# A selective scan over sixteen states: four of sixteen B products move to ScalarE and TensorE

## The reference

```python
xc, z = split(x @ in_w.T); xc = silu(causal_conv4(xc) + conv_b)       # 128 channels each
dt, Bm, Cm = split(xc @ x_w.T)                                        # rank 4, 16 states, 16 states
dt = softplus(dt @ dt_w.T + dt_b); A = -exp(A_log)
dA  = exp(dt[..., None] * A)                                          # token, 128 channels, 16 states
dBx = dt[..., None] * Bm[:, :, None, :] * xc[..., None]
h_t = dA_t * h_{t-1} + dBx_t
y_t = sum_s h_t[:, s] * C_t[s]
y = (y + xc * D) * silu(z);  out = y @ out_w.T
```

## Time and profile before

| | |
|---|---|
| median of 3 runs | 2970.94 us (2959.31 to 2975.59) |
| profiled execution, its own time | 2967.89 us |
| its span, first to last instruction | 2966.1 us |
| busy over the span | PE 84%, POOL 70%, DVE 78%, ACT 53% |
| mean granted TensorE clock | 0.899 of full speed |
| forward direction | about 815 to 1722 us from the span's start |
| backward direction | about 1730 to 2692 us |

### The profile page before, as it was taken

One profiled execution on the slowest core, in us unless ns is written; L12 is line 12 of the kernel. 1 busy time (PEld: TensorE's weight loads), 2 busy tenths in 40 slices (PEclk: granted clock), 3 DMA queues, 4 the chain that ended last, 5 costly groups with the idle time before them and its releaser, 6 DMA issues. The chain is left out here.

```text
span 2966.1 us, 34800 instructions
## 1 busy us (share of the span) xinstructions
PE 2497.7 (84%) x7800; PEld 1190.2 (40%) x7800; DVE 2318.3 (78%) x2487; ACT 1576.8 (53%) x2784; POOL 2084.2 (70%) x1166
## 2 busy tenths in 40 slices
PE   7899999957468988889889858899889889988598
PEld 7666666624322323323323223333333333336422
DVE  4366666560659999999999939998999899895499
ACT  6466666543655655555656446555555555545221
POOL 3133333230359999999999949999999999995155
PEclk6699999969779999999999889999999999997599
DMA  3000000000256777777777637776766676660022
GB/s 60 8 9 9 9 9 9 6 1 0 59 167 223 243 244 237 247 235 240 246 236 241 227 124 235 219 236 216 229 226 222 221 225 224 218 211 17 13 54 47
DMA packets 177295, 437.72 MB, mean 148 GB/s; under 512 B 65638, under 2 KB 70219, under 8 KB 177228
## 3 DMA queue, kind: packets, MB, share of 16 engines
q1 hardware_dynamic: 139340, 420.19, 44.5%
q10 hardware_dynamic: 37888, 16.79, 2.1%
HBM read 404.40 MB, written 24.12 MB: 144 GB/s over the span
## 5 line engine op out<-in xcount | busy, mean ns | idle before, releaser
L1443 POOL TENSOR_TENSOR sb_hc<-sb_h,sb_cc 128x1024 f32<-128x1024 f32 x256 | 599.7, 2360 | 61.8 <-PE sb_py L1232 56.2
L1443 POOL TENSOR_TENSOR sf_hc<-sf_h,sf_cc 128x1024 f32<-128x1024 f32 x256 | 595.8, 2347 | 11.5 <-DVE sf_h L1521 8.2
L1232 PE MATMUL sf_py<-sf_hc,ident 128*128 128x512 f32 x1024 | 533.1, 655 | 0.6 <-POOL sf_hc L1443 0.6
L1232 PE MATMUL sb_py<-sb_hc,ident 128*128 128x512 f32 x1024 | 519.5, 638 | 0.0
L572 POOL TENSOR_TENSOR ar_sc<-ar_sc,ar_mx 128x512 f32<-128x512 f32 x128 | 154.7, 1208 | 356.6 <-DVE ar_mx L513 356.6
L1521 DVE TENSOR_TENSOR_SCAN sf_h<-sf_dA,sf_state,sf_pu 128x1024 f32<-128x1024 f32 x160 | 375.4, 2346 | 19.1
L1521 DVE TENSOR_TENSOR_SCAN sb_h<-sb_dA,sb_state,sb_pu 128x1024 f32<-128x1024 f32 x160 | 375.2, 2345 | 17.1
L1232 PEld LDWEIGHTS sf_py<-sf_hc,ident 128*128 128x128 f32 x1024 | 197.0, 205 | 269.3 <-issue 239.8
L1232 PEld LDWEIGHTS sb_py<-sb_hc,ident 128*128 128x128 f32 x1024 | 187.3, 196 | 241.0 <-issue 232.0
L1501 DVE TENSOR_TENSOR sb_pu<-sb_pu,sb_dtx 128x1024 f32<-128x1024 f32 x160 | 193.9, 1212 | 52.7 <-PE sb_pu L1212 52.7
L1436 POOL TENSOR_TENSOR sb_dbx<-sb_dtx,sb_bb 128x1024 f32<-128x1024 f32 x96 | 226.5, 2359 | 3.3 <-DVE sb_dtx L1482 3.3
(11 more groups left out here) (294 smaller groups left out, 4594.6 us busy)
## 6 DMA issues: line engine op xcount, KB each, us to landing
sf_cc<-rows_scratch SPq DMA_DIRECT2D x256, 512.0 KB, 4.4
sb_cc<-rows_scratch SPq DMA_DIRECT2D x256, 512.0 KB, 4.4
sf_bb<-rows_scratch SPq DMA_DIRECT2D x96, 512.0 KB, 5.4
sb_bb<-rows_scratch SPq DMA_DIRECT2D x96, 512.0 KB, 5.4
sf_n<-n_scratch SPq DMA_DIRECT2D x32, 258.0 KB, 5.4
sb_n<-n_scratch SPq DMA_DIRECT2D x32, 258.0 KB, 5.3
y_scratch<-sf_yo SPq DMA_DIRECT2D x16, 512.0 KB, 6.1
sb_yf<-y_scratch SPq DMA_DIRECT2D x16, 512.0 KB, 5.1
```

The source lines that it names most:

```text
L1232: ins = nc.tensor.matmul(p_y[:, hf], lhsT=c.ident[:, :], rhs=hc[:, s % RING, hf], start=False, stop=(s == U - 1))
L1443: nc.gpsimd.tensor_tensor(hc[:, s % RING, :], h[:, s % RING, :], cc[:, s % C_RING, :], ALU.mult).then_inc(read, 1)
```

## The change

Of the sixteen inputs dt*x*B, VectorE now makes eight (BY_V), GpSimd four (BY_G) and ScalarE four (BY_A = 3, 5, 9, 12). For ScalarE's, tokens have to be on partitions: TensorE computes B with tokens on partitions (columns_b: eight matmuls of 128x128 weights and 16 columns) and turns dtx (turn_x: eight transposes of 128x128), ScalarE copies both out of p_p (take_columns_b, take_turned_x). For each of the four states ScalarE makes eight copies of 128x128 scaled by a column of B (scale, three units ahead) into sT, and TensorE turns them back into p_u[s % 2] (turn_in, eight transposes) in the place where a spread would stand. The decays of BY_A go into the ring dA, now of four tiles. The last column of h is kept for two states at once. bb has one tile instead of three, and the dbx ring two. store_parts and load_parts move to units 12 and 14, step_size to 6 and 6, backward gate_in to 5 and 5, project to 14, take_z to 6, add_x to 15.

```diff
-C_RING, B_RING, DECAY_RING = 4, 3, 5
-DECAY_AHEAD, INJECT_AHEAD, LAG_SUM = 3, 2, 4
-BY_G = (2, 5, 7, 10, 13, 15)
-BY_V = tuple(s for s in range(16) if s not in BY_G)
+C_RING, B_RING, DECAY_RING, TURN_RING = 4, 2, 4, 2
+DECAY_AHEAD, INJECT_AHEAD, SCALE_AHEAD, LAG_SUM = 3, 2, 3, 4
+BY_V = (1, 2, 4, 7, 8, 11, 13, 15)
+BY_A = (3, 5, 9, 12)
+BY_D = tuple(sorted(BY_V + BY_A))
+BY_G = tuple(s for s in range(STATES) if s not in BY_D)
...
+            def columns_b(m, par):
+
+                pe.wait_ge(r_copied, m + 1)
+                for j in range(BLOCKS):
+                    ins = nc.tensor.matmul(p_p[:, j * STATES:(j + 1) * STATES], lhsT=xc[:, par, j * Q:(j + 1) * Q],
+                                           rhs=k["bc"][:, 0:STATES], start=True, stop=True)
+                ins.then_inc(bt_made, 1)
+
+            def turn_x(m, par):
+
+                pe.wait_ge(dtx_done, m + 1)
+                for j in range(BLOCKS):
+                    ins = nc.tensor.transpose(p_p[:, j * Q:(j + 1) * Q], dtx[:, par, j * Q:(j + 1) * Q], c.ident[:, :])
+                ins.then_inc(x_turned, 1)
+
+            def turn_in(n, par, s):
+
+                r = BY_A.index(s)
+                pe.wait_ge(scaled, n * NA + r + 1)
+                need(pe, scanned, n * U + s - 1)
+                for j in range(BLOCKS):
+                    ins = nc.tensor.transpose(p_u[s % 2][:, j * Q:(j + 1) * Q], sT[:, (par * NA + r) % TURN_RING, j, :], c.ident[:, :])
+                ins.then_inc(turned_in, 1)
...
             prepare = [(0, convolve(a)), (0, convolve(b)), (2, in_out(a)), (3, in_out(b)),
-                       (5, step_size(a)), (6, step_size(b))]
+                       (4, columns_b), (6, step_size(a)), (6, step_size(b)), (13, turn_x)]
             if back:
-                run(pe, unit, prepare, [(13, project)], [(4, gate_in(a)), (4, gate_in(b))])
+                run(pe, unit, prepare, [(14, project)], [(5, gate_in(a)), (5, gate_in(b))])
...
+            def take_columns_b(m, par):
+                act.wait_ge(bt_made, m + 1)
+                nc.scalar.copy(bT[:, par, :, :].rearrange("p j s -> p (j s)"), p_p[:, 0:BLOCKS * STATES]).then_inc(bt_taken, 1)
+
+            def take_turned_x(m, par):
+                act.wait_ge(x_turned, m + 1)
+                need(act, scaled, NA * m)
+                nc.scalar.copy(dtxT[:, :, :].rearrange("p j d -> p (j d)"), p_p[:, :]).then_inc(xt_taken, 1)
+
+            def scale(n, par, s):
+                r = BY_A.index(s)
+                if r == 0:
+                    act.wait_ge(bt_taken, n + 1)
+                    act.wait_ge(xt_taken, n + 1)
+                need(act, turned_in, n * NA + r + 1 - TURN_RING)
+                for j in range(BLOCKS):
+                    ins = nc.scalar.activation(sT[:, (par * NA + r) % TURN_RING, j, :], dtxT[:, j, :], ACT.Copy,
+                                               scale=bT[:, par, j, s:s + 1])
+                ins.then_inc(scaled, 1)
...
-                act.wait_ge(scanned, n * U + s + 1)
+                act.wait_ge(scanned, n * U + s + 2)
                 e = 0 if back else TC - 1
-                nc.scalar.copy(state[:, s:s + 1], h[:, s % RING, e:e + 1]).then_inc(kept, 1)
+                nc.scalar.copy(state[:, s:s + 2], h[:, s % RING:s % RING + 2, e]).then_inc(kept, 1)
...
-                       (8, softplus_exp), (8, softplus_one), (8, softplus_log), (9, part_middle), (11, store_parts),
-                       (11, take_dt), (12, load_parts)]
+            prepare = [(1, silu_x), (4, bc_rows), (5, load_flat), (5, take_columns_b), (6, part_high), (7, softplus_relu),
+                       (7, softplus_abs), (8, softplus_exp), (8, softplus_one), (8, softplus_log), (9, part_middle),
+                       (11, take_dt), (12, store_parts), (14, take_turned_x), (14, load_parts)]
...
-                need(sp, g_injected, n * NG_ + r + 1 - B_RING)
-                spread_row(bb[:, r % B_RING, :], n, s, b_spread[r % B_RING])
+                need(sp, g_injected, n * NG_ + r)
+                spread_row(bb[:, :], n, s, b_spread)
```

More of the change, by code:

```diff
@@ L1111, in scan_direction @@
             sem(s) for s in ("r_copied", "r_stored", "f_loaded", "high", "remained", "middle", "lowest", "p_stored"))
+        bt_made, bt_taken, x_turned, xt_taken, scaled, turned_in = (
+            sem(s) for s in ("bt_made", "bt_taken", "x_turned", "xt_taken", "scaled", "turned_in"))
         p_loaded = [sem("p_loaded%d" % j) for j in range(2)]
@@ L1114, in scan_direction @@
         c_spread = [sem("c_spread%d" % j) for j in range(C_RING)]
-        b_spread = [sem("b_spread%d" % j) for j in range(B_RING)]
+        b_spread = sem("b_spread")
         block = ctx.enter_context(nc.Block())
@@ L1127, in past @@
         def past(order, n, s, ring):
-            r = order.index(s) - ring
-            return n * U + order[r] + 1 if r >= 0 else (n - 1) * U + order[r + len(order)] + 1
+            r = order.index(s)
+            if r >= ring:
+                return n * U + order[r - ring] + 1
+            return (n - 1) * U + order[max(q for q in range(len(order)) if q % ring == r % ring)] + 1
         def run(eng, unit, prepare=(), tail=(), own=()):
@@ L1162, in step @@
                 def step(m, par, last):
-                    pe.wait_ge(r_copied, NC if last else m + 2)
+                    pe.wait_ge(bt_taken, NC if last else m + 2)
                     if last:
-                        pe.wait_ge(dt_done, NC)
-                        pe.wait_ge(dtx_done, NC)
+                        pe.wait_ge(xt_taken, NC)
                     ins = nc.tensor.matmul(p_p[:, hf], lhsT=k["z"][:, :],
@@ L1240, in project @@
                 pe.wait_ge(y_gated, m + 1)
-                pe.wait_ge(dt_done, NC if last else m + 3)
-                pe.wait_ge(dtx_done, NC if last else m + 3)
+                pe.wait_ge(xt_taken, NC if last else m + 3)
                 pe.wait_ge(z_copied, NC if last else m + 2)
@@ L1255, in unit @@
                     spread_b(m, mpar, ms)
+                if ms in BY_A and not (last and s == U - 1):
+                    turn_in(m, mpar, ms)
                 if s >= LAG_SUM:
@@ L1383, in unit @@
                 if first and s == 0:
+                    if s in BY_G:
+                        decay_g(0, 0, s)
                     for j in range(DECAY_AHEAD):
-                        if j in BY_V:
+                        if j in BY_D:
                             decay_v(0, 0, j)
+                    for j in range(SCALE_AHEAD):
+                        if j in BY_A:
+                            scale(0, 0, j)
                 m, mpar, ms = after(n, par, s + 1)
@@ L1389, in unit @@
                     decay_g(m, mpar, ms)
+                if s % 2 and s >= 3:
+                    keep(n, s - 3)
+                elif s % 2 and not first:
+                    keep(n - 1, s - 3 + U)
                 m, mpar, ms = after(n, par, s + DECAY_AHEAD)
-                if ms in BY_V and not (last and s + DECAY_AHEAD >= U):
+                if ms in BY_D and not (last and s + DECAY_AHEAD >= U):
                     decay_v(m, mpar, ms)
-                if s >= 2:
-                    keep(n, s - 2)
-                elif not first:
-                    keep(n - 1, s - 2 + U)
+                m, mpar, ms = after(n, par, s + SCALE_AHEAD)
+                if ms in BY_A and not (last and s + SCALE_AHEAD >= U):
+                    scale(m, mpar, ms)
             act.wait_ge(zeroed, 1)
-            prepare = [(1, silu_x), (4, bc_rows), (5, load_flat), (6, part_high), (7, softplus_relu), (7, softplus_abs),
-                       (8, softplus_exp), (8, softplus_one), (8, softplus_log), (9, part_middle), (11, store_parts),
-                       (11, take_dt), (12, load_parts)]
+            prepare = [(1, silu_x), (4, bc_rows), (5, load_flat), (5, take_columns_b), (6, part_high), (7, softplus_relu),
+                       (7, softplus_abs), (8, softplus_exp), (8, softplus_one), (8, softplus_log), (9, part_middle),
+                       (11, take_dt), (12, store_parts), (14, take_turned_x), (14, load_parts)]
             exp_log_tables()
             if back:
-                run(act, unit, prepare, [(1, silu_z)], [(1, exp_log_tables), (5, take_z)])
+                run(act, unit, prepare, [(1, silu_z)], [(1, exp_log_tables), (6, take_z)])
                 silu_z(NC - 1, 1, True)
@@ L1528, in _ @@
             run(dve, unit, [(9, lost), (10, step_sum), (12, dt_x)],
-                [(LAG_SUM - 1, gate), (14, add_x)] if back else [])
+                [(LAG_SUM - 1, gate), (15, add_x)] if back else [])
             if back:
```

39 lines of the change are left out of this document (23 added, 16 removed).

## The result

The changed kernel takes 3010.65 us (median of 4 runs, 3005.53 to 3018.92) against 2965.12 (2951.19 to 2975.59) for the kernel before, run beside it: ratio 1.016, 95% interval 1.011 to 1.021. The forecast of 3049 had the sign and the engine; the time lies in its range (3005 to 3100), 38 us under its centre and 6 over its low end.

What follows compares the result with a forecast made beforehand. GpSimd bounds forward, no engine is full backward; TensorE's full stretch, units 0 to 7, decides the change. 15 x (2.6 + 2.8) = 81, less 3, on 2967.9 gives 3046; plus 3, 3049 us. Range 3005 to 3100.

Steps and rivals of the forecast that it cites:

- The bound and the sign: TensorE, full from unit 0 to the product of state 8, gets more work: slower, chance 0.83.
- The two parts of a chunk: Chunk cut at scan 15's end and state 8's product: forward first part 25.06 to 29.5 us, second 28.87 to 27.0.
- GpSimd's and VectorE's relief: Each loses two products a chunk, of 2.31 us on GpSimd and 1.34 on VectorE.
- columns_b: TensorE, unit 4: eight matmuls priced from project at 2.4 us.
- A turn: Eight TensorE transposes taken at 1.0 us, between 0.94 and 1.09.
- The first part: From scan 15's end to state 8's product, set by TensorE: 29.5 us forward, 33.8 backward.
- The second part: From state 8's product to the next scan 15's end: one VectorE product fewer, wait for GpSimd's sum may go, 27.0 us.
- The sum: 15 chunks a direction at +2.6 forward and +2.8 backward, 81 us; last chunks and lead-in -3; so +78.
- the signs that I had named: Chunk lengths, TensorE without idle in units 0 to 7, VectorE's waits of 5 to 7 us, GpSimd under 180, both prices.
- It is covered: GpSimd stalls about 3 us a chunk for state 12's row of C; its 52.3 us stay under the chunk's 56.5.
- The first rival: GpSimd or ScalarE late as well: +1.5 us in each second part, 3094 us; chance 0.18.
- I take that they are not late: The loaded parts, wanted by unit 0's spread two units behind load_parts, arrive in time and add nothing.

Runs made afterwards that it cites:

- 5: The changed kernel with SyncE issuing the row of C before the row of B, and one of eight matmuls in columns_b: 2957.53 us, ratio 0.998.
- 6: The changed kernel with SyncE issuing the row of C before the row of B, and one of eight transposes in each turn: 2965.67 us, ratio 1.000.
- experiment 1: The changed kernel with SyncE issuing a state's row of C before the row of B that waits for bb: 2998.82 us, ratio 1.012.
- C first: Same run as experiment 1: the changed kernel with the row of C issued before the row of B, 2998.82 us, ratio 1.012.

## Why the prediction was right, and where its sizes were off

**The bound and the sign: right.** VectorE waited for TensorE at the products of states 7 and 8, TensorE had no idle time from unit 0's spread to unit 7, and both kinds of work put there are paid when the DMA waits are away (5: 41 us, 6: 33 us). The two parts of a chunk moved as forecast, in opposite directions: the first from 25.06 to 28.5, the second from 28.87 to 26.4. GpSimd's and VectorE's relief is real, and lies in the part that was not the problem.

**columns_b: 2.4 forecast, 1.70 measured.** The row I priced it from, project at 2.48, had run partly at the lower clock (0.68 from 2155.1 to 2157.5), like the total beside it that the same group shows. In the changed kernel project takes 1.73 (2372.05 to 2373.78). Both are 16 records at 0.107 us. The bound that I had taken as the low one, 1.87 from the transposes' spacing, was still too high. A turn: 1.0 forecast, 0.93 measured (0.88 elsewhere).

**The first part: 29.5 forecast, 28.5 measured; backward 33.8 and 32.3.** Of the 1.0 forward, 0.7 is columns_b and 0.14 the two turns. Backward the 0.7 that project was to come late is gone as well, with project at 1.73. **The second part: 27.0 forecast, 26.4 measured.** The scans' wait for GpSimd's sum was gone, as hoped for, and a bit more.

**The sum.** From the last lead-in to the last chunk, the fifteen intervals forward grew by 22.6 us in all and the backward ones by 23.0 (the start of the first lost to that of the last, 844.53 to 1665.74 against 841.01 to 1639.59; 1774.10 to 2650.02 against 1751.52 to 2604.45): 46 where the forecast had 81. But the mean hides where they come from. The first backward interval alone grew by 9.0 (51.23 against 42.21) and the first forward one by 4.6, where the sum had 2.8 and 2.6 for them as for every other; why was not tried. The fourteen others of a direction grew by 18.0 forward and 14.0 backward: 1.3 and 1.0 us a chunk, less than half of the 2.6 and 2.8 forecast. What lies outside the intervals grew by 5 where I had -3: of 51.0 us between the spans, 45.6 are inside. Of those outside, 3.4 lie before the first convolve (819.49 and 822.87) and 6.4 from the start of the experts block on (2696.06 and 2740.66), which the change doesn't touch. The lead-in forward grew by 0.1 where I had 3, and from the last lost of a direction on, the rest of forward with the lead-in of backward shrank by 3.6, the rest of backward by 1.0 where I had 4.6.

**How much of it was luck.** The direction and the place were forecast and shown. But the time is in the range by 6 us only. Had the two first intervals grown like the others, by 1.3 and 1.0 instead of 13.6 together, it would lie near 2999, below the range; and of the 51.0 us between the profiled executions 9.8 lie in stages that the change doesn't touch. Of the signs that I had named, three held (TensorE without idle time, VectorE's waits at those two products, a turn near 1.0). The chunks of 56 to 57 and 60 to 61.5 us did not come (55.56 and 58.97), nor did a columns_b near 2.4; VectorE's 5 to 7 us of waits came backward alone, and GpSimd came under 180 of 200 backward (171) and just missed it forward (180.75).

**"It is covered": half right.** The stall behind the row of B was 4.3 us, not 3, and with it GpSimd came to scan 0 up to 2.2 us late; experiment 1 prices this, with the parts of B and three falls of the clock, at 12 us or 0.4 us a chunk. The first rival had the mechanism and the wrong place: it was to bind in the second part by 1.5 us a chunk, and it bound at scan 0, by 0.4.

**"I take that they are not late": wrong.** The loaded parts were late in 8 of 11 chunks, by 0.1 to 0.6 us each. I had looked at which unit waits for them and not at how long they take: 6.9 us where the same load took 3.2 in the kernel before. The rows that the one bb holds back and that are then issued together don't explain it: with C first, where GpSimd no longer waits for a row of C, the load still took 6.3. In both, the DMA engines were full while it ran; it now stands at unit 14 and not at 12. Which of the two makes it slow was not tried.

**The clock.** The rule of the Trainium skill, page "TensorE: Matmul & The Clock Gate", section "Part 4: PE-mode transpose", would have had no full clock in the turns: in the changed kernel's windows, which hold the turns, the granted clock is 1.00, and a turn takes 0.93, below the 1.0 taken from the earlier trace rows. The trace disagrees with the page, as the earlier trace rows did. What I left out is the other direction: the clock was not at its upper level throughout in the kernel before (0.94 forward and 0.96 backward over whole chunks), so its TensorE prices were no constants, and the changed kernel got part of that back (0.99 and 1.00).

**The waits of VectorE** came to 2.9 us forward and 5.4 backward at the two products, where 5 to 7 were forecast; the difference is the cheaper first part.

## What to carry to other kernels

Cut the loop body at the points where two engines meet, and price a change in each part by itself: here each engine had time over by its average, and the added work cost its full length since it went to the one part in which its engine was full. With the rows of C issued first, one state moved, and the columns made where the engine idles in the forward direction, the same change turned from 1.6% slower to 1.3% faster. When undoing one part of a change brings less than its work, sort the loop bodies by length and look at what the long ones have in common before giving up the theory: here it was not the wait that the profile named, but the clock. Where a wait stands, ask what would have held the engine without it. And never take a price from a record without reading the granted clock over it.

## What the runs showed of the hardware

- Short idle times of TensorE, 0.25 to 1.8 us each, were followed in part of the chunks by the lower clock for a few microseconds (0.72 in the mean of six), which cost 1.7 us where TensorE was the bound. In the run of 5 nine of fourteen forward chunks had such a fall, seven of them at unit 0, and the others did not, with the same work before them. Nineteen matmuls of zeros a chunk, in the idle places, took the fall away in fourteen of fourteen, and their TensorE time (4.9 us a chunk, 1.50 + 0.83 + 1.06 + 1.50 by their groups) cost nothing.
- Taking work from TensorE could slow its clock. Forward chunks of fourteen in which the total of unit 0 was slow: 3 in the changed kernel, 11 with one matmul of the columns, 7 with one transpose; with C first 0, then 7 and 8.
- float32 matmuls with 128x128 weights and few moving columns took the time of their weight loads: 0.107 us a record with 16 columns and with 64 alike (16 records in 1.70 and 1.73 us), with fifteen weight loads in 1.75 us without a gap beside them, against 0.45 with 512 (a total, four records in 1.81).
- A 96 KB load took 6.9 us from issue to landing in the changed kernel and 6.3 with C first, with a DMA share of 1.0 while it ran, and 3.2 in the kernel before (share 0.73 in 1384 to 1388). The store of the same 96 KB two units or less before it took 1.8 us in the first two and 5.4 in the last.
- ScalarE's 128x128 scale with its factor from a tile took 387 ns, eight of them 2.43 us, so 0.29 from start to start: one starts before the last has ended.
